# A Hadamard-fused feed-forward on eight Trainium2 cores: transforming the hidden activations instead of the down-projection weights

## What is computed

```python
x = x + attention(layernorm(x))          # 16 heads of 128, causal, D = 2048
h = silu(ln(x) @ W1.T) * (ln(x) @ W3.T)  # hidden width 8192
h = fwht(h)                              # Walsh-Hadamard over 8192, times 1/sqrt(8192)
x = x + h @ W2.T                         # back to 2048
```

## Time and profile before

| | us |
|---|---|
| median of 3 runs (lowest, highest) | 4312.96 (4047.42, 4434.35) |
| the profiled execution | 4038.11 |
| its span, cores 0 to 7 | 4017.8 to 4036.3 |
| busy in the span: PE, DVE, ACT, POOL | 2701.0, 948.8, 629.0, 226.6 |
| granted TensorE clock, mean of each core | 0.832 to 0.835 |

### The profile page before, as it was taken

The page is one execution under the profiler, slowest core; times in us unless marked ns, Lnnn a source line. Parts: engine busy times, 40 slices in busy tenths (PEclk is TensorE's granted clock), DMA queues, the critical chain, the costliest instruction groups (busy, mean ns, idle before and its releaser), DMA issues.

```text
span 4035.8 us, 35222 instructions; the slowest of 8 cores (4017.8 to 4036.3 us)
## 1 busy us (share of the span) xinstructions
PE 2701.0 (67%) x12544; PEld 1216.7 (30%) x12544; DVE 948.8 (24%) x1347; ACT 629.0 (16%) x852; POOL 226.6 (6%) x237
## 2 busy tenths in 40 slices
PE   1158769778697697714999999994001333697796
PEld 0123414334244252312444444442000000243342
DVE  4614132141331312043001010115884000000001
ACT  1113122121221222101000000000001344100000
POOL 0000000000000001000111111110000000000000
PEclk9998879889798798856999999997555555798898
DMA  3230220202202104533888888882004999765665
GB/s 121 84 42 1 32 32 1 32 1 32 32 1 32 26 7 54 90 107 32 78 78 74 76 80 75 75 78 26 0 0 81 174 178 182 148 145 146 148 144 156
DMA packets 564629, 292.28 MB, mean 72 GB/s; under 512 B 433264, under 2 KB 547952, under 8 KB 558320
## 3 DMA queue, kind: packets, MB, share of 16 engines
q0 software_dynamic: 356112, 134.76, 31.0%
q1 hardware_dynamic: 208352, 155.29, 15.4%
HBM read 374.43 MB, written 50.33 MB: 105 GB/s over the span
## 4 chain that ended last, share of the span: by engine, by line
PE 57%; DMA 20%; DVE 16%; issue 3%; ACT 2%; DVEq 0%; SPq 0%; POOL 0%; ACTq 0%; POOLq 0%
PE pfd L680 11%; PE pfd L673 11%; PE pfd L806 6%; PE pfd L342 6%; DMA w2p<-arena 6%; DMA arena<-w2p 6%; PE pfd L393 6%; PE pfd L429 3%; PE pfd L437 3%; DVE arena L718 3%; DVE arena L723 3%; DMA arena<-wk 3%; PE pfd L556 3%; PE pfd L369 3%; DVE arena L501 3%
## 5 line engine op out<-in xcount | busy, mean ns | idle before, releaser
L673 PE MATMUL pfd<-arena 128*128 128x512 bf16 x2048 | 777.4, 380 | 9.9 <-DMA arena<-w1t 9.9
L680 PE MATMUL pfd<-arena 128*128 128x512 bf16 x2048 | 777.3, 380 | 3.7 <-DMA arena<-w3t 3.7
L746 PE MATMUL pfd<-arena 128*128 128x512 bf16 x256 | 134.4, 602 | 543.8 <-DMA arena<-w2t 407.9
L806 PE MATMUL pfd<-arena 128*128 128x512 bf16 x2048 | 453.5, 382 | 61.0 <-DMA arena<-w2p 61.0
L342 PE MATMUL pfd<-arena 128*128 128x512 bf16 x1024 | 240.4, 400 | 145.2 <-DMA arena<-wk 145.2
L806 PEld LDWEIGHTS pfd<-arena 128*128 128x128 bf16 x2048 | 198.6, 98 | 315.8 <-issue 88.4
L697 DVE TENSOR_TENSOR arena<-arena,pfd 128x512 bf16<-128x512 bf16 x128 | 88.0, 688 | 811.6 <-ACT arena L689 811.6
L673 PEld LDWEIGHTS pfd<-arena 128*128 128x128 bf16 x2048 | 200.6, 98 | 251.3 <-issue 11.2
L680 PEld LDWEIGHTS pfd<-arena 128*128 128x128 bf16 x2048 | 200.6, 98 | 248.1 <-issue 7.9
L462 ACT ACTIVATE arena<-pfd 128x1024 bf16<-128x1024 f32 x192 | 196.4, 1023 | 410.0 <-PE pfd L452 404.8
L256 PE MATMUL pfd<-arena 128*128 128x128 bf16 x384 | 44.8, 309 | 294.7 <-DVE arena L244 294.7
(11 more groups left out here) (57 smaller groups left out, 1826.9 us busy)
## 6 DMA issues: line engine op xcount, KB each, us to landing
arena<-w1t POOLq DMA_DIRECT2D x64, 512.0 KB, 9.0
arena<-w3t POOLq DMA_DIRECT2D x64, 512.0 KB, 11.0
arena<-w2t POOLq DMA_DIRECT2D x64, 512.0 KB, 8.0
w2p<-arena SPq DMA_DIRECT2D x64, 512.0 KB, 9.2
arena<-x SPq DMA_DIRECT2D x24, 1024.0 KB, 5.8
arena<-wq POOLq DMA_DIRECT2D x8, 1024.0 KB, 10.1
arena<-wk POOLq DMA_DIRECT2D x8, 1024.0 KB, 14.3
arena<-wv POOLq DMA_DIRECT2D x8, 1024.0 KB, 18.4
```

The lines of the kernel that those rows point to most:

```text
L673: lambda e, _b=gate_b, _dc=dc, _qb=qb, _buf=buf: e.matmul(pf(_b)[:, :], w1_sv[_buf][:, _dc * 128:(_dc + 1) * 128], xln2T3[:, _dc, _qb * 51 ...
L680: lambda e, _b=lin_b, _dc=dc, _qb=qb, _buf=buf: e.matmul(pf(_b)[:, :], w3_sv[_buf][:, _dc * 128:(_dc + 1) * 128], xln2T3[:, _dc, _qb * 512 ...
L746: lambda e, _b=bank, _ns=ns, _buf=buf: e.matmul(pf(_b)[:, :], h128_s[:, :], w2s[_buf][:, _ns * 512:(_ns + 1) * 512], start=True, stop=True),
L806: lambda e, _b=bank, _hb=hb, _buf=hbuf, _s=slot, _qb=qb: e.matmul(pf(_b)[:, :], colh[_buf][:, (_hb % 32) * 128:((_hb % 32) + 1) * 128], hs ...
```

## The change

It edits the feed-forward alone. The scratch tensor w2p and the whole stage that transforms W2 go. The butterfly becomes a helper, `emit_bfly`, that is called three times: after block 31 of the up-projections for the first 5 levels of blocks 0 to 31 (160 operations), after block 63 for those of blocks 32 to 63 (160 operations), and for the last level over all (64 operations). A new stage then multiplies every slot of the activations by the Hadamard matrix on PE (2 matmuls of 512 columns) and writes it back in place, scaled, on ACT (one operation of 128x1024). The down-projection loads its pieces from w2t itself, on POOL instead of SP: 128 partitions x 32 pieces of 128 numbers, 512 bytes read and 256 written each. In the code below `slot_last_v` is the count of the DVE instruction that wrote a slot last.

```diff
-    w2p_hbm = nc.dram_tensor("w2p", [NHB, 16, 128, 128], BF16, kind="Internal").ap()
...
+        def emit_bfly(indices, dists):
+            for dd in dists:
+                for i0 in range(indices[0], indices[-1] + 1, 2 * dd):
+                    for i in range(i0, i0 + dd):
+                        a_s, b_s = loc[i], loc[i + dd]
+                        f_s = bf_state["spare"]
+                        V1 = emit("vector", ...)
+                        V2 = emit("vector", ...)
+                        slot_last_v[f_s] = V1
+                        slot_last_v[a_s] = V2
+                        loc[i], loc[i + dd], bf_state["spare"] = f_s, a_s, b_s
+            return cnt["V"]
...
+            if hb == 31:
+                emit_bfly(list(range(0, 32)), [1, 2, 4, 8, 16])
+        emit_bfly(list(range(32, 64)), [1, 2, 4, 8, 16])
+        V_h64_done = emit_bfly(list(range(0, 64)), [32])
...
-        preset(["w2s0", "w2s1", "w2p0", "w2p1"])
-        for hb in range(NHB):
-            W_s = emit("gpsimd", ... w2s <- w2t_h[hb * 128:(hb + 1) * 128, :])
-            for ns in range(4):  T_f = emit("tensor", ... matmul(pf(bank), h128_s, w2s))
-            for ns in range(4):  S_e = emit("scalar", ... activation(w2p, Copy, scale=FW_SCALE))
-            ST_w = emit("sync", ... w2p_hbm[hb] <- w2p)
+        for i in range(NHB):
+            slot = loc[i]
+            for half in range(2):
+                bank = 2 * (i % 2) + half
+                T_h1 = emit("tensor",
+                            lambda e, _i=i, _s=slot, _h=half: e.matmul(
+                                PF[_i % 2][:, _h * 512:(_h + 1) * 512], h128_s[:, :],
+                                hslot(_s, _h * 512, (_h + 1) * 512),
+                                start=True, stop=True),
+                            waits=g_wait(f"pbank{bank}") +
+                                  ([("V", slot_last_v.get(slot, V_h64_done))]
+                                   if half == 0 else []),
+                            inc="T")
+            S_h128 = emit("scalar",
+                          lambda e, _i=i, _s=slot: e.activation(
+                              out=hslot(_s, 0, TQ), in_=PF[_i % 2][:, :],
+                              func=AF.Identity, scale=FW_SCALE),
+                          waits=[("T", T_h1)], inc="S")
...
                     L_half[half] = emit(
-                        "sync",
+                        "gpsimd",
                         lambda e, _hb=hbuf, _doc=doc, _h=half: e.dma_start(
                             out=colh[_hb][:, :].rearrange("p (hb t) -> p hb t", hb=32),
-                            in_=w2p_hbm[_h * 32:(_h + 1) * 32, _doc].rearrange(
-                                "hb p t -> p hb t")),
-                        waits=list(ST_w2p) + g_wait(f"colh{hbuf % 2}"), inc=f"Lch{hbuf % 2}", n=16)
+                            in_=w2t_src[:, _h * 32:(_h + 1) * 32,
+                                        _doc * 128:(_doc + 1) * 128]),
+                        waits=g_wait(f"colh{hbuf % 2}"), inc=f"Lch{hbuf % 2}", n=16)
...
-                                                       ("V", V_h64_done)]
+                                                       ("S", S_h128_done)]
```

More of the change, by code:

```diff
@@ L651, in build_nc @@
         w3_src = w3t_h.rearrange("(dc p) n -> p dc n", p=128)
+        loc = list(range(NHB))
+        bf_state = {"spare": NHB}
+        slot_last_v = {}
+        def emit_bfly(indices, dists):
[4 more added lines that the diff above has]
+                        f_s = bf_state["spare"]
+                        V1 = emit("vector",
+                                  lambda e, _a=a_s, _b=b_s, _f=f_s: e.tensor_tensor(
+                                      out=hslot(_f, 0, TQ), in0=hslot(_a, 0, TQ),
+                                      in1=hslot(_b, 0, TQ), op=ALU.add),
+                                  inc="V")
+                        V2 = emit("vector",
+                                  lambda e, _a=a_s, _b=b_s: e.tensor_tensor(
+                                      out=hslot(_a, 0, TQ), in0=hslot(_a, 0, TQ),
+                                      in1=hslot(_b, 0, TQ), op=ALU.subtract),
+                                  inc="V")
+                        slot_last_v[f_s] = V1
+                        slot_last_v[a_s] = V2
+                        loc[i], loc[i + dd], bf_state["spare"] = f_s, a_s, b_s
+            return cnt["V"]
         for hb in range(NHB):
@@ L706, in build_nc @@
                     g_set(f"silu{buf}", "V", V_h)
+            if hb == 31:
+                emit_bfly(list(range(0, 32)), [1, 2, 4, 8, 16])
+        emit_bfly(list(range(32, 64)), [1, 2, 4, 8, 16])
+        V_h64_done = emit_bfly(list(range(0, 64)), [32])
         ar.free("w1_s"); ar.free("w3_s"); ar.free("silu0"); ar.free("silu1")
         ar.free("xln2T")
-        loc = list(range(NHB))
-        spare = NHB
-        d = 1
-        while d < NHB:
-            for i0 in range(0, NHB, 2 * d):
-                for i in range(i0, i0 + d):
-                    a_s, b_s = loc[i], loc[i + d]
-                    emit("vector",
-                         lambda e, _a=a_s, _b=b_s, _f=spare: e.tensor_tensor(
-                             out=hslot(_f, 0, TQ), in0=hslot(_a, 0, TQ),
-                             in1=hslot(_b, 0, TQ), op=ALU.add),
-                         inc="V")
-                    emit("vector",
-                         lambda e, _a=a_s, _b=b_s: e.tensor_tensor(
-                             out=hslot(_a, 0, TQ), in0=hslot(_a, 0, TQ),
-                             in1=hslot(_b, 0, TQ), op=ALU.subtract),
-                         inc="V")
-                    loc[i], loc[i + d], spare = spare, loc[i], loc[i + d]
-            d *= 2
@@ L769, in build_nc @@
-        ST_w2p = [("SW0", cnt["SW0"]), ("SW1", cnt["SW1"])]
-        ar.free("w2s0"); ar.free("w2s1"); ar.free("w2p0"); ar.free("w2p1")
+        S_h128 = None
+        for i in range(NHB):
+            slot = loc[i]
+            T_h1 = None
+            for half in range(2):
[14 more added lines that the diff above has]
+                          waits=[("T", T_h1)], inc="S")
+            for half in range(2):
+                g_set(f"pbank{2 * (i % 2) + half}", "S", S_h128)
@@ L772, in build_nc @@
+        S_h128_done = S_h128
         preset(["colh0", "colh1", "o2T", "outb0", "outb1"])
+        w2t_src = w2t_h.rearrange("(hb p) n -> p hb n", p=128)
         ar.alloc("colbuf", 2 * 32 * 128 * 2, side="top")
```

37 lines of the change are left out of this document (removed).

## The result

The changed kernel took 3887.3 us in the median of its runs (lowest 3877.0), the kernel before 4047.3 beside it; the ratio is 0.9599, 95% interval 0.9583 to 0.9615. So it is faster by 4.0%. Forecast were 3838 us, a gain of 200; the gain was 160.

What follows compares the result with a forecast made beforehand. Four hardly overlapping stages: PE bounds the up- and down-projections, DVE the butterfly, DMA the W2 transform. 4038.1 - 377.8 - 22.4 + 39 + 91.7 - 19.3 + 88.3 = 3837.6 us, 3838; range 3730 to 4040.

Steps and rivals of the forecast that it cites:

- The W2 stage goes: Between butterfly and down-projection: the removed transform of W2 takes 377.8 us off.
- the Hadamard product stays behind the butterfly: Ahead of the down-projection: 33 ACT operations are left after the last DVE operation, +39 us.
- the move gains 22: Up-projections: moving 160 butterfly operations takes 127.3 us away, less a 102.4 us PE stall and 2.5 cold start: 22.4 gained.
- The rival that POOL starves: Up-projections: POOL can't issue block 33's loads during the moved butterfly, 24 us more, 3862 us; chance 0.06.
- the cycle of the down-projection: Down-projection, a buffer's load and use: 11.1 + 9.55 = 20.65 us per output block, against 14.9 before.
- the clock holds: Rival, down-projection: PE stays at full clock despite waiting for loads, cycle 18.2 us, 3760 us; chance 0.22.
- Landing plus cold half: Down-projection cycle: a load landing in 11.1 us plus 32 matmuls starting at half clock, 9.55 us.
- first half: Down-projection, first sixteen output blocks: 337.5 us against 245.8 before, +91.7.
- second half: Down-projection, second sixteen output blocks: 326.4 us against 238.1 before, +88.3.
- the gap between the halves: Down-projection: loads on POOL no longer wait behind output stores, PE goes on at some 3731 instead of 3750.32, -19.3 us.
- Loads as quick as those of w2p: Rival, down-projection: loads take 7.05 us and the stage stays bound by PE at 14.15, 3643 us; chance 0.04.
- The slow queue: Rival, down-projection: loads land as late as 20.6 us, cycle 30.2, 4123 us; decides from 27.3 us; chance 0.05.

Runs made afterwards that it cites:

- e8: The kernel before with only its down-projection loads taken from w2t, cast, on POOL, the W2 transform still running unused: 4272 and 4283 us, against 4029 to 4041 before.

## Why the prediction was right and where it was off

*The W2 stage goes, the Hadamard product stays behind the butterfly, the move gains 22.* These three were -361.2 in the sum. From the first load of w1t to the first load of the down-projection it is 1220.3 us after and 1584.3 before: -364.0. The timeline of the seam:

```profile
2333.37 0.69 DVE L721 TENSOR_TENSOR arena<-arena,pfd 128x512 bf16<-128x512 bf16 x1 [6.16 <-ACT arena L713]
2334.16 0.69 DVE L663 TENSOR_TENSOR arena<-arena 128x1024 bf16<-128x1024 bf16 x1
...
2461.49 3.06 DVE L721 TENSOR_TENSOR arena<-arena,pfd 128x512 bf16<-128x512 bf16 x4
```

Behind the last multiplication of block 31 stand 127.3 us of butterfly, and four multiplications have piled up by then. PE stood still for 102.0 us of it (the page's L704 row), 102.4 in the sum. PE started again at half clock. The exposed end of the Hadamard product is 39.3 us for 39. The experiment with the butterfly put back confirms the move by itself (20 to 26 for 22).

*The rival that POOL starves* falls. POOL's timeline in the midst of the butterfly:

```profile
2346.75 1.14 POOL L681 DMA_DIRECT2D arena<-w1t  x1 [11.55 <-PE pfd L704]
2347.89 1.15 POOL L681 DMA_DIRECT2D arena<-w3t  x1
```

These loads go out as soon as PE has freed the buffer and take the usual 1.14 us, with DVE at work throughout. The Trainium skill ("SBUF — State Buffer", SBUF: two separate sides) counts a DVE operation with two SBUF inputs only against a GpSimd operation that reads SBUF; these 1.14 us agree.

*The step that was off: the cycle of the down-projection.* The mechanism held. There is one idle piece of 5 to 6 us per output block, and the clock falls in it. Slices of 1 us from the pause ahead of 3199.19, where PE starts again, show it (clock in the third column from the right):

```profile
3195.00:3196.00 1.00, 0.00 (x0) 0.00 (x0) 0.00 (x0) 0.00 (x0) 1.00 (x1) 1.00 1.80 180
3196.00:3197.00 1.00, 0.00 (x0) 0.00 (x0) 0.00 (x0) 0.00 (x0) 0.31 (x1) 0.57 1.59 157
3198.00:3199.00 1.00, 0.00 (x0) 0.00 (x0) 0.00 (x0) 0.00 (x0) 0.00 (x0) 0.50 1.40 126
3203.00:3204.00 1.00, 1.00 (x6) 0.47 (x5) 0.00 (x0) 0.00 (x0) 0.00 (x0) 1.00 1.39 137
```

That is the rival *the clock holds* answered, against it. But the size was 20.65 us in the sum and 21.41 and 21.68 in the trace of the two halves. Landing plus cold half were right together, 20.71 for 20.65, but each by itself was off by some 0.4 us the other way (11.50 for 11.1, 9.21 for 9.55); that they cancel is luck. The idle piece was put at 4 to 5 us and is 5 to 6. What I left out are 0.70 us between them, POOL waking behind PE's last matmul (0.51) and PE waking behind the landing (0.14 and a little), which come back in every cycle. At 15 cycles in the first half and 14 in the second (from 3514.70 to 3818.26) the cycle's excess is +11.4 and +14.4 us.

The other part lies at the ends. The first load took 15.96 us from issue to landing, where I took 11.1 from the first loads of the up-projections: +5. That is this core's: on the others the same load took 18.2 (core 1), 12.6 (core 4) and 10.1 to 11.2 us. The first load that POOL issues in the second half, for its second block, took 21.42 us beside the last store of the output and a load of the residual on SP's queue; from the first block's start to the second's it is 29.9 us, +9.3. Here all cores agree: the load behind the gap took 15.6 to 21.6 us on the eight. That SP's traffic is the cause is inferred from the coincidence, no run has tried it without. I had written that the gap between the halves goes from 51.5 to about 32 us, since POOL has both buffers full. It did, from 3450.65 to 3484.76 it is 34.1; but the collision with SP's traffic came a block later, and I had not asked what the loads that POOL issues *after* the gap would meet.

The bill, after minus forecast, by profiled executions: first load of w1t 8.4 later (nothing there was touched), up to the first load of the down-projection -2.8, first half +15.7 (353.2 for 337.5), between the halves +1.9, second half +24.1 (350.5 for 326.4), behind it -5.7, outside the span -0.2. That is +41.4, and 3837.6 + 41.4 = 3879.0.

*The other rivals.* Loads as quick as those of w2p (7.05 us) didn't come: the fastest of 64 took 10.0. The Trainium skill's formula in "DMA: Bandwidth & Descriptors" (Anatomy of one DMA) gives 4.4 or 6.8 us here; an estimate that the runs don't bear out for such pieces (11.3 us in the median, 10.0 at best). The slow queue, 27 us per cycle, did not come either, though the two loads of 17.4 and 18.4 us in e8 and the one of 21.4 here show that it exists for a load or two.

## What to carry to other kernels

When a stage depends on "load, use, load again" through two buffers, write its cycle as landing + use + the wake-ups between them, and multiply by the number of cycles before trusting a figure taken from the fastest nearby load; if the sum exceeds the use of both buffers, look at the loads first: here smaller loads into more buffers and wider pieces gained, matmuls put into the engine's pauses lost. Long work that is put into the list of an in-order engine between two pipelined stages costs its length minus what the consumer can run ahead; in pieces shorter than one block's slack the same work cost PE nothing here. And what a removed transform saved must be set against the layout it had produced: here 196.8 us of tail, more than half of the 378, went back into loads that read twice the bytes, cast them and land later.

## What the runs showed of the hardware that I had not expected

- Matmuls put into the pauses kept the clock up and still lost time: landings of the same 1 MB loads went from 11.3 us in the median to 13.3 and 14.2, the tail from 780 to 815 and 826 us, on the slowest cores.
- More loads in flight lengthened each. A third 1 MB buffer brought 15.9 to 20.5 us instead of 11.3; six buffers of 512 KB instead of four, 19.6 instead of 12.4. The third buffer still shortened the tail, to between 619 and 724 us; the six gained nothing clear of the noise.
- With the third buffer the cores went apart, spans of 3690 to 3814 us in the profiled execution and 3714 to 3796 in the other; in the changed kernel they are within 34 us. The same code and loads gave one core 125 GB/s and another 100.
- The DMA share can exceed 1.0 far: 1.01 in the changed kernel, 1.43 with quarters, 1.25 with twice the width, though at 148 GB/s instead of 128. It isn't a measure of how full the path is.
